# Computing each row of the expanded image once: kept rows, a new table of jobs, and wider blocks

## What is computed

```python
# layer 0: windows of 8x8 pixels, 9 nearest neighbours of each pixel in its window
y = affine(conv1x1(x, fc1_w, fc1_b)); nodes = windows(y)          # 64 nodes of 96 channels
idx = top_k(-dist(nodes), 9)                                      # itself and 8 others
h = gelu(affine(concat(x_i, x_j - x_i) @ ew.T + eb)); h = max over the 9 neighbours
x = affine(conv1x1(h, fc2_w)) + x
# layer 1
h = relu(bn(w1 @ x))                    # 96 -> 576 channels, a product per pixel
h = relu(bn(depthwise 3x3(h)))          # 9 taps, one row of padding above and below
out = x + bn(w2 @ h)                    # 576 -> 96 channels
```

## Time and profile before

| what | value |
|---|---|
| median of 3 runs | 4356.01 us (4351.47 to 4366.89) |
| the profiled execution, its time | 4357.96 us |
| its span | 4356.3 us |
| PE busy | 4092.7 us, 94% |
| DVE busy | 4082.7 us, 94% |
| ACT busy | 3609.4 us, 83% |
| POOL busy | 493.5 us, 11% |

### The profile page before, as it was taken

How to read it: one execution, slowest core, us unless ns; L and a number is a source line. 1 busy time by engine, 2 the same in 40 slices (tenths; PEclk the granted TensorE clock), 3 DMA queues, 4 the chain that set the end, 5 groups by cost and what they waited for, 6 DMA issues and landing times.

```text
span 4356.3 us, 84124 instructions
## 1 busy us (share of the span) xinstructions
PE 4092.7 (94%) x26688; PEld 2421.8 (56%) x26688; DVE 4082.7 (94%) x5296; ACT 3609.4 (83%) x7141; POOL 493.5 (11%) x548
## 2 busy tenths in 40 slices
...
GB/s 47 23 30 34 27 41 21 29 38 32 33 29 33 25 37 32 25 45 18 32 38 32 33 29 34 25 34 36 25 40 20 35 32 25 45 17 25 30 21 24
DMA packets 52989, 134.11 MB, mean 31 GB/s; under 512 B 7778, under 2 KB 9058, under 8 KB 46372
## 3 DMA queue, kind: packets, MB, share of 16 engines
...
...
## 4 chain that ended last, share of the span: by engine, by line
PE 64%; DVE 14%; issue 12%; ACT 8%; DVEq 0%; DMA 0%; SPq 0%; ACTq 0%; POOL 0%; POOLq 0%
PE pg L568 15%; DVE acc L950 10%; PE pmisc L494 8%; PE pg L571 7%; PE pmisc L478 7%; PE pvu L555 6%; PE pmisc L439 3%; PE pself L582 3%; PE pmisc L446 3%; PE pmisc L461 3%; ACT MV L742 2%; PE pmisc L463 2%; DVE hid L937 2%; PE pmisc L496 2%; PE pvu L541 2%
## 5 line engine op out<-in xcount | busy, mean ns | idle before, releaser
L950 DVE SCALAR_TENSOR_TENSOR acc<-hpad,w,acc 128x1024 f32<-128x1024 f32 (+1 forms) x2560 | 2927.2, 1182 | 56.6 <-ACT acc L775 56.3
L568 PE MATMUL pg<-MV,VU 128*128 128x512 f32 x2048 | 1146.9, 642 | 46.7 <-ACT VU L750 40.0
L759 ACT ACTIVATE g<-pg 128x512 f32<-128x512 f32 x1536 | 920.2, 599 | 114.3 <-PE pg L571 59.6
L937 DVE TENSOR_REDUCE hid<-g 128x192 f32<-128x1728 f32 x512 | 998.2, 1950 | 0.0
L742 ACT ACTIVATE MV<-pvu,cst 64x512 f32<-64x512 f32 x1024 | 697.4, 681 | 9.8 <-PE pvu L541 0.2
L478 PE MATMUL pmisc<-x,w 96*128 96x384 f32 (+1 forms) x1536 | 581.2, 490 | 22.5 <-ACT hpad L689 17.7
L571 PE MATMUL pg<-MV,VU 128*64 128x512 f32 x2048 | 527.5, 592 | 0.0
L494 PE MATMUL pmisc<-acc,w 128*96 128x256 f32 x2048 | 494.9, 385 | 30.7 <-ACT acc L782 30.7
L689 ACT ACTIVATE hpad<-pmisc,sh,sc 128x384 f32<-128x384 f32 (+1 forms) x768 | 485.5, 664 | 25.9 <-DVE acc L950 15.9
L555 PE MATMUL pvu<-wVU,y 97*64 97x192 f32 x4096 | 446.6, 339 | 32.6 <-ACT MV L742 32.2
L494 PEld LDWEIGHTS pmisc<-acc,w 128*96 128x96 f32 x2048 | 332.0, 165 | 214.3 <-issue 111.0
...
## 6 DMA issues: line engine op xcount, KB each, us to landing
...
x<-in_x_dram POOLq DMA_DIRECT2D x128, 192.0 KB, 3.6
res<-x POOLq DMA_DIRECT2D x128, 192.0 KB, 3.6
out_dram<-res SPq DMA_DIRECT2D x128, 192.0 KB, 2.1
...
```

What stands on the lines that cost most here:

```text
L568: last = nc.tensor.matmul(ps[:, :], VU[:, r, part, 0:ONE128], cols[part], start=True, stop=True)
L759: nc.scalar.activation(g[:, p % 2, part, :, 0:KN], pg[(3 * p + part) % 2][:, :].rearrange("p (n k) -> p n k", k=KN), ACT.Gelu).then_inc(ge ...
L937: nc.vector.tensor_reduce(hid[:, c % 2, j, :, :], g[:, r], op=ALU.max, axis=AX.X).then_inc(hid_ready, 1)
L950: nc.vector.scalar_tensor_tensor(out=dst, in0=src, scalar=wk, in1=dst, op0=ALU.mult, op1=ALU.add).then_inc(tap_done, 1)
```

## The change

Each row of `w1`'s output is computed once. A strip's jobs make the 16 rows below its first two, as two jobs of 8 rows (512 columns) for a full group and one job for the half group. The strip's first two rows are the last two of the strip above, and are copied: for the full groups by POOL (`keep`, 2 x 66 numbers on 128 partitions), for the half group by two DMAs of SP (`UPPER_AT`, `LOWER_AT`), since these rows go from one half of the partitions to the other. At an image's top a zero row takes their place, and a third, one-row job (`m == 2`) makes row 0. New semaphores `kept` and `kept_half` order the copies against ACT's writes and `tap0`; a copy itself waits for the last tap of the strip above. The jobs of an image go from 98 to 83.

All tables are new. `fc1` and `ssq` were in slots 1 to 6 and 17 to 22, and are now spread over the whole image, at most one of each in a slot. `w2` goes from offsets 12, 13, 14, 16 to 12, 14, 15, 16. `tap0` of group 2 goes from the end of offset 2 to the early place at offset 4. `TAP_COUNTS` is evened out.

```diff
-FC1_AT = {1: 0, 2: 1, 4: 2, 5: 3}
-SSQ_AT = {2: 0, 3: 1, 5: 2, 6: 3}
+FC1_AT = {5: (0, 7), 6: (1, 0), 13: (1, 1), 14: (1, 2), 21: (1, 3), 22: (1, 4), 29: (1, 5), 30: (1, 6)}
+SSQ_AT = {2: (0, 5), 3: (0, 6), 6: (0, 7), 10: (1, 0), 18: (1, 1), 19: (1, 2), 22: (1, 3), 26: (1, 4)}
...
-W1_AT = {-1: [(0, 0), (0, 1), (0, 2)], 0: [(1, 0), (1, 1)], 1: [(1, 2), (2, 0)],
-         2: [(2, 1), (2, 2), (3, 0)], 3: [(3, 1), (3, 2), (4, 0)], 4: [(4, 1)]}
-TAP0_AT = {5: [4]}
-TAP0_LATE = {0: [0], 1: [1], 2: [2], 4: [3]}
+W1_AT = {-1: [(0, 0), (0, 1), (0, 2)], 0: [(1, 0)], 1: [(1, 1), (1, 2)], 2: [(2, 0), (2, 1), (2, 2)],
+         3: [(3, 0), (3, 1), (3, 2), (4, 0), (4, 2)]}
+KEEP_AT = {-2: (0, 1), 2: (2, 3)}
+UPPER_AT, LOWER_AT = {2: FULL}, {4: FULL}
+TAP0_AT = {4: [2], 5: [4]}
+TAP0_LATE = {0: [0], 1: [1], 4: [3]}
 RELU2_AT = {6: [0], 7: [1], 10: [2], 11: [3, 4]}
-W2_AT = {12: 0, 13: 1, 14: 2, 16: 3}
-TAP_COUNTS = [5, 4, 4, 6, 4, 5, 6, 6]
+W2_AT = {12: 0, 14: 1, 15: 2, 16: 3}
+TAP_COUNTS = [5, 4, 5, 5, 5, 5, 6, 5]
...
+            def keep(t, s, gr):
+                if due(count := tap_number(s - 1, gr, TAPS - 1)):
+                    pool.wait_ge(tap_done, count)
+                pool.sem_inc(pool_passed, 1)
...
+                    nc.gpsimd.tensor_copy(hpad[:, gr, 0:2, :], hpad[:, gr, STRIP:STRIP + 2, :]).then_inc(kept, 1)
...
+                        elif m == 1:
+                            act.wait_ge(kept, FULL * s + gr + 1)
...
+            def tap0(b, p, o, t, s, gr):
+                if gr < FULL:
+                    act.wait_ge(kept, FULL * s + gr + 1)
+                else:
+                    act.wait_ge(kept_half, 32 * s + 32)
```

More of the change, by code:

```diff
@@ L58, in w1_slot, with w1_last @@
     return next(o for o, parts in W1_AT.items() if (gr, m) in parts)
+def w1_last(t, gr):
+    return (gr, 2 if t == 0 else 1 if gr < FULL else 0)
 def due_in(table, b, p):
@@ L78, in misc_jobs @@
     q = p % 16
-    if valid(bi, B):
-        if q in FC1_AT:
-            jobs.append(("fc1", bi, c0 + FC1_AT[q]))
-        if q in SSQ_AT:
-            jobs.append(("ssq", bi, c0 + SSQ_AT[q]))
-        if q in INV_AT:
-            jobs.append(("inv", bi, c0 + INV_AT[q]))
+    first = isinstance(b, int) and b < 0
+    for kind, table in (("ssq", SSQ_FIRST if first else SSQ_AT), ("fc1", FC1_FIRST if first else FC1_AT)):
+        if p in table:
+            ahead, c = table[p]
+            if valid(b + ahead, B):
+                jobs.append((kind, b + ahead, c))
+    if q in INV_AT and valid(bi, B):
+        jobs.append(("inv", bi, c0 + INV_AT[q]))
     if p % 4 == 1:
@@ L92, in misc_jobs @@
     for _, t, s, parts in due_in(W1_AT, b, p):
-        jobs += [("w1", t, s, part) for part in parts]
+        jobs += [("w1", t, s, part) for part in parts if part[1] < 2 or t == 0]
     jobs.sort(key=lambda job: ORDER.index(job[0]))
@@ L147, in bank_free @@
         return MISC
-    n = jobs_in(b - 1) if b >= 0 else 0
-    earlier = [j for j in range(n) if j % MISC == i % MISC]
-    return i + n - earlier[-1] if earlier else i + 1
+    backs = []
+    for n in [] if b < 0 else [jobs_in(0), jobs_in(1)] if b == 1 else [jobs_in(b - 1)]:
+        backs += [i + n - j for j in range(n) if j % MISC == i % MISC][-1:]
+    return min(backs, default=i + 1)
 def when(b, p, ago):
@@ L274, in build @@
             "vu_ready", "vu_evac", "gather_ready", "self_ready", "gelu_done", "self_gelu"))
+        kept, kept_half = sem("kept"), sem("kept_half")
         sp_passed, pool_passed, dve_passed = sem("sp_passed"), sem("pool_passed"), sem("dve_passed")
@@ L411, in image @@
                         inverse_norms(b, p, bi, h)
+                    for o, t, s, groups in due_in(KEEP_AT, b, p):
+                        for gr in groups:
+                            keep(t, s, gr)
                     for o, t, s, q in due_in(ADD_AT, b, p):
```

95 lines of the change are left out of this document (50 added, 45 removed).

## The result

The changed kernel took **4436.16 us** (median of 4 runs, 4427.66 to 4437.98) beside 4355.31 us for the kernel before: a ratio of 1.0177, 95% interval 1.0154 to 1.0201. It is slower, and outside the range given (4250 to 4368); 4322 had been predicted.

What follows compares the result with a forecast made beforehand. PE with ACT was taken to bound heavy halves and DVE light ones; afterwards PE with ACT, 259.2 us an image (261.9 with branch, against 263.81). Saving 2.1 x 16 = 34 us gives 4356 - 34 = 4322 us, range 4250 to 4368.

Steps and rivals of the forecast that it cites:

- Prices: PE's time per job, start to next start: w2 2.16 us, fc2 1.73, a 512-column w1 job 0.86.
- The chain in slot 4: Slots 4, 12, 20, 28: relu2, w2, emptying, tap0, onehot, values in series; 9.7 us instead of 6.93, 11.1 an image.
- the second rival: Light halves: DVE late, chain longer, slots 12 and 28 take 1.2 us more each; 4360, no change; chance 0.15.
- The third rival: POOL's copies block DVE at 0.53 us each, DVE gets slower; 38 us slower, 4394; chance 0.12.
- A one-row job has no row; I take 0.25: PE's price in us for a 64-column job, between nothing and 0.645; said to matter in five jobs an image.
- The branch: The loop's branch, in an image's last light half: 2.7 us instead of 2.0 in a PE without slack.
- Waits that are added, and why I cost them at nothing: Waits for the keep copies and half-group DMAs, held to be covered by earlier slots and idle POOL: no cost.
- POOL beside DVE: A 132-number POOL copy beside DVE's taps takes 0.53 us and costs DVE 0.14, 2.2 us an image.
- The sum over PE: Per image, PE with ACT needs 248.1 us plus 11.1, 259.2, beside DVE's 255.7; the larger decides.
- the first rival: The chain in slot 4 is not real and DVE binds: 85 us faster, up to 120; 4255; chance 0.13.

Runs made afterwards that it cites:

- e14_w2_taps: e8_part_tail with the w2 jobs at their old offsets 12, 13, 14, 16 and the old counts of taps: 4279.00 us, ratio 0.9839.
- e4_before_spread: The kernel before with the new tables of fc1 and ssq alone: 4278.29 us, ratio 0.9835.
- e11_double_copy: e1_part with each POOL copy of kept rows made twice: 4322.99 us beside 4322.37.
- e1_part: The changed kernel with a slot's only job behind the second gather product instead of ahead of expand: 4322.37 us, ratio 0.9935.
- e8_part_tail: e1_part with the kept rows of the last image's tail copied by DVE instead of POOL: 4296.73 us, ratio 0.9867.
- e16_after_w2: The changed kernel with the w2 jobs alone back at their old offsets 12, 13, 14, 16: 4406.72 us, ratio 1.0120.
- e12_w2_old: e8_part_tail with the w2 jobs at their old offsets 12, 13, 14, 16: 4266.83 us, ratio 0.9800.
- e13_bunched_w2: e1_part with fc1 and ssq in their old slots and the w2 jobs at their old offsets: 4371.85 us, ratio 1.0040.

## Why the prediction was wrong

**Prices, right.** Two weight loads of `w1` in the tail stand 0.43 us apart, and a job of 512 columns has two, 0.86, as taken:

```profile
4302.50 0.19 PEld L519 LDWEIGHTS pmisc<-x,w 96*128 96x128 f32 x1 [0.24 <-issue]
4302.93 0.19 PEld L519 LDWEIGHTS pmisc<-x,w 96*128 96x128 f32 x1 [0.24 <-issue]
```

PE's work fell by 50 us of the 69 (4.3 an image) that were worked out, an evacuation of 512 was 780 ns, under its bound of 0.90, and the 22 other slots of 32 came within 0.35 us.

**The chain in slot 4, right in 4 and 20, low in 12 and 28.** 9.87 against 9.70 there. For 12 the same figure was used, with no look at slot 11, whose bottom-edge evacuations make ACT late (+1.1), and with the clock taken as full (+0.5 in the mean). In 28 `feature_square` waits for DVE as the second rival had it, and the clock falls too: +0.8. That rival named these slots and 2.4 us an image; they gave 2.5. In mechanism it was the nearest of the three, though it ended at 4360. The third rival's 4394 is nearer in time, but its cause, blocked taps, did not occur: that nearness is luck.

**Slot 19, low by 0.9.** "A one-row job has no row; I take 0.25". Two of them stand in this slot with three jobs of 512 and an `ssq`, and their evacuations are 0.40 us each on ACT, while only three banks are there to wait in. Slot 19 of image 8 in after (L524 is the half group's job, L721 empties the first one-row job, L515 is the second):

```profile
2331.37 1.08 PE L524 MATMUL pmisc<-x,w 96*64 96x512 f32 x4
...
2332.72 0.40 ACT L721 ACTIVATE hpad<-pmisc,sh,sc 128x64 f32<-128x64 f32 x1
2332.88 0.19 PEld L515 LDWEIGHTS pmisc<-x,w 96*64 96x64 f32 x2 [1.31 <-ACT hpad L732]
```

The job's price on PE was small, as said (0.33 us busy for its two products); the wait for a bank was not. Slot 19 stayed at 9.6 to 9.8 in every kernel with spread tables and one-row jobs but e14_w2_taps (10.4), and was 8.2 in e4_before_spread, which has none of these jobs. No run took these jobs alone out of the changed kernel.

**The branch, low.** Taken at 2.7 us of a branch image, it was 3.5 to 4.0 in slot 31 in five of six branch images (12.2 to 12.7 against 8.7) and, by the clock, up to 3 more in slot 0.

These are most of the excess of an image: +1.6 and +0.8 in slots 12 and 28, +0.9 in 19, and about +1.5 at the branch beyond what was allowed, 4.8 of 267.1 - 260.6 = 6.5 us; the rest is small excesses in slots like 3, 11 and 27. Over 14 images that is 91 of the 114 us by which the prediction missed.

**"Waits that are added, and why I cost them at nothing", wrong in the tail.** The covers named for `keep` were all slots of the loop, where POOL is idle and DVE pauses for other work between taps. They held there; the trace has two waits of ACT for a copy, 18.8 and 20.4 us, both in the tail (its timeline above). At the program's end there is no other work; DVE runs 23 and 40 taps in a row, and the copy that frees `w1`'s next evacuation gets no turn. This cost 24 us, and no step of the prediction looked at the stretch behind the last pair.

**"POOL beside DVE", wrong in who waits.** The copy was priced at 0.53 us and its cost to DVE at 0.14. The copy took 1.21 us in the mean and up to 20.98, and DVE paid 0.04 us for it (e11_double_copy). The 0.14 belongs to the other copy: in after as before, the 120 taps in which an `xs` copy of 512 numbers ends take 1.42 us. The prediction set the rule of the Trainium skill ("SBUF — State Buffer", SBUF: two separate sides), that a GpSimd operation and a VectorE operation with two SBUF inputs lock each other out, against the row with the tap of 1.42 us, and read it as a loss for DVE. The tail's rows agree with the rule that they exclude each other, and show which side loses here: a 132-number copy beside 18 taps in a row took 20.98 us, twice. The third rival, in which the copies block DVE, fell with it.

**The sum over PE, and DVE "beside it".** The prediction took the larger of two sums over an image, 259.2 for PE with ACT and 255.7 for DVE. e1_part tests this without the chain: PE's sum is then 248.1 and DVE's 255.7, so that the first rival should have come, 4255 to 4271 by its own terms. It came to 259.1 an image, 3.4 over DVE's sum, and with the tail mended as well to 4297 (e8_part_tail). As I read the windows, the sums don't bind by the image but in turns: DVE in slots 10 to 14, PE in 15, 0 and 19. A `w2` moved from 13 to 15, and its three likes in the other strips, is neutral in both sums and costs 2.4 us an image in e8_part_tail. In the changed kernel itself its undoing gave 30 us (e16_after_w2), though the lengths of these slots had been predicted well one by one: what the model lacked was where the other engine is late, and so where work is free.

**What the idea itself is worth.** e12_w2_old has each row of `w1` computed once and e4_before_spread has it twice, both with spread tables and the old places of `w2`: 4266.83 against 4278.29, ratios whose intervals just don't touch (0.9816 and 0.9818). But the two differ in the counts of taps as well; with the old counts in both, it is 4279.00 (e14_w2_taps) against 4278.29. So 50 us less work on PE bring at most about 11 us, with the tail's copies on DVE, and nothing with the old counts. With `fc1` and `ssq` in the old places e13_bunched_w2 is 17 us over the kernel before, less than the tail's 24, so there too the idea is worth a few us. Spreading `fc1` and `ssq` brings 74. The changed kernel had that gain and lost it again: the chain 114 us, the place of `w2` 30, the tail 25.
